# Row-sum and mean-square reciprocals: from VectorE's reciprocal to Exp of minus Ln on ScalarE

## The reference, cut to what matters

```python
def attn(x, gamma, w_qkv, w_out):          # layers 0 and 1
    ...
    qkv = jnp.einsum('bnc,fc->bnf', xn, w_qkv)
    ...
    sim = jnp.where(causal_mask, neg, jnp.einsum('bihd,bjhd->bhij', q, k))
    attn = jax.nn.softmax(sim, axis=-1)    # row sums: the first changed reciprocal
    out = jnp.einsum('bhij,bjhd->bihd', attn, v)
    return jnp.einsum('bnf,cf->bnc', out.reshape(b, n, 1024), w_out)

def L1_ffn(x, ...):                        # last stage, three blocks
    for blk in range(3):
        y = qlora_linear(h, ...)           # base + bias + LoRA
        mu = mean(y); var = mean((y - mu) ** 2)
        y = (y - mu) * rsqrt(var + 1e-5) * g + b   # the second changed one
        y = jax.nn.gelu(y, approximate=False)
        h = qlora_linear(y, ...) + h
    return h

x = x + layernorm(attn0(layernorm(x)))
x = x + layernorm(int8_matmul(layernorm(x)))
x = x + layernorm(attn1(layernorm(x)))
x = x + layernorm(L1_ffn(layernorm(x)))
```

## Time and profile before

| what | us |
|---|---|
| three runs | 4528.47, 4347.83, 4516.64 |
| median | 4516.64 |
| profiled execution, its own time | 4341.71 |
| its span on the slowest core (6) | 4340.2 |
| spans of the eight cores | 4296.7 to 4340.2 |
| attention of layer 0, phase B with its last out_groups | about 565 to 1590 |
| attention of layer 1, the same | about 2375 to 3376 |
| last stage | 3376 to 4340 |

### The profile page before, as it was taken

How to read it: one execution, slowest core, us unless ns; L and a number is a source line. 1 busy time by engine, 2 the same in 40 slices (tenths; PEclk the granted TensorE clock), 3 DMA queues, 4 the chain that set the end, 5 groups by cost and what they waited for, 6 DMA issues and landing times.

```text
span 4340.2 us, 45815 instructions; the slowest of 8 cores (4296.7 to 4340.2 us)
## 1 busy us (share of the span) xinstructions
PE 3411.5 (79%) x16411; PEld 1414.8 (33%) x16736; DVE 2637.4 (61%) x4777; ACT 2032.6 (47%) x2339; POOL 906.7 (21%) x868
## 2 busy tenths in 40 slices
PE   4888946787999945548998467899897379978997
PEld 1333322232333312223443123333332134433443
DVE  5666457666644458865555676655444466586457
ACT  1111113466777726662333135667784255436443
POOL 2222200000011003225565000000000123234333
PEclk8878767899999968778999689999998689989999
DMA  5111021113111044426566111111101500031004
GB/s 171 49 49 59 15 92 49 49 59 85 58 48 48 31 133 144 140 76 172 177 176 181 53 62 51 44 44 40 39 20 38 197 25 25 15 135 50 1 1 146
DMA packets 93476, 330.50 MB, mean 76 GB/s; under 512 B 12416, under 2 KB 16000, under 8 KB 88384
## 3 DMA queue, kind: packets, MB, share of 16 engines
q1 hardware_dynamic: 93248, 327.56, 22.9%
HBM read 228.94 MB, written 98.57 MB: 75 GB/s over the span
## 4 chain that ended last, share of the span: by engine, by line
PE 52%; DVE 35%; ACT 6%; DMA 3%; issue 3%; SPq 0%; POOL 0%; DVEq 0%; POOLq 0%; ACTq 0%; another core or an unknown queue 0%
PE pp L764 8%; PE pp L649 8%; PE pp L790 8%; DVE s_rcp L830 6%; PE pp L853 6%; PE pp L654 5%; PE pp L1316 4%; PE pp L807 3%; PE pp L1271 3%; ACT f_yg L1303 2%; PE pp L633 1%; DVE s_bst L859 1%; DVE s_y L860 1%; DVE s_x L866 1%; DVE f_r L1295 1%
## 5 line engine op out<-in xcount | busy, mean ns | idle before, releaser
L773 ACT ACTIVATE s_probs<-pp,s_negM 128x1024 bf16<-128x1024 f32 (+2 forms) x1152 | 1141.7, 1040 | 772.8 <-PE pp L764 765.2
L790 PE MATMUL pp<-s_probs,s_v 128*128 128x512 bf16 (+3 forms) x2271 | 667.5, 376 | 91.8 <-DVE s_feat L832 78.5
L764 PE MATMUL pp<-s_q,s_kT 128*128 128x512 bf16 (+3 forms) x2219 | 664.9, 380 | 31.2 <-DMA s_q<-qspill 17.0
L830 DVE RECIPROCAL s_rcp<-pp 128x512 f32<-128x512 f32 x128 | 429.7, 3357 | 126.3 <-PE pp L827 122.2
L780 POOL TENSOR_SCALAR_AFFINE_SELECT s_probs<-s_probs 128x256 bf16<-128x256 bf16 x256 | 107.9, 422 | 1682.8 <-ACT s_probs L773 1671.2
L853 PE MATMUL pp<-s_wq,s_feat 128*128 128x512 bf16 x1003 | 290.4, 439 | 153.2 <-DVE s_rcp L830 96.1
L1271 PE MATMUL pp<-f_h,f_w 128*128 128x512 bf16 x1501 | 364.3, 390 | 16.1 <-ACT f_h L1246 13.9
L807 PE MATMUL pp<-s_probs,ones 128*32 128x512 bf16 (+4 forms) x2302 | 247.1, 384 | 126.1 <-DVE s_lo L820 124.3
L790 PEld LDWEIGHTS pp<-s_probs,s_v 128*128 128x128 bf16 x2304 | 225.3, 101 | 355.9 <-DVE s_feat L832 91.6
L1281 POOL TENSOR_TENSOR f_sq<-f_yg 128x512 bf16<-128x512 bf16 x192 | 210.6, 1097 | 579.4 <-ACT f_yg L1276 573.3
L764 PEld LDWEIGHTS pp<-s_q,s_kT 128*128 128x128 bf16 x2304 | 195.7, 102 | 323.9 <-issue 128.3
(11 more groups left out here) (182 smaller groups left out, 5168.4 us busy)
## 6 DMA issues: line engine op xcount, KB each, us to landing
s_x<-x SPq DMA_DIRECT2D x64, 512.0 KB, 4.0
xbuf<-s_x SPq DMA_DIRECT2D x64, 512.0 KB, 2.6
s_fqi<-qwT SPq DMA_DIRECT2D x48, 512.0 KB, 5.1
s_fsc<-scT SPq DMA_DIRECT2D x48, 512.0 KB
qspill<-s_qst SPq DMA_DIRECT2D x16, 1024.0 KB, 7.1
s_q<-qspill SPq DMA_DIRECT2D x16, 1024.0 KB, 4.9
m_x<-xbuf SPq DMA_DIRECT2D x32, 512.0 KB, 5.0
xbuf<-m_x SPq DMA_DIRECT2D x32, 512.0 KB, 2.6
```

The costliest lines, as they stand in the source:

```text
L764: s_tok[i] = PE(lambda e, kc=kc, q0=q0, c0=c0, b=b, h=h, qt=qt: e.matmul(PS[b][:, c0:c0 + 512 - q0], S.kT[:, h, kc * 128:(kc + 1) * 128], ...
L773: tok = AC(lambda e, b=b, w=w, sl=sl, h=h, qt=qt: e.activation(S.probs[:, sl, 0:w], PS[b][:, 0:w], AF.Exp, bias=S.negM[:, h, qt:qt + 1], s ...
L790: tok = PE(lambda e, kc=kc, q0=q0, c0=c0, sl=sl, h=h, po=po, first=first, last=last: e.matmul(po[:, q0:512], S.v[:, kc, h * 128:(h + 1) * ...
L830: r = DV(lambda e: e.reciprocal(S.rcp[:, k, :], MISC), t)
```

## The change

The row sums' reciprocal leaves DVE: ACT takes Ln of MISC into `rcp`, then Exp with scale -1 in place. MISC is free after Ln. The multiply into `feat` waits for Exp. In the last stage Sqrt becomes Ln and the DVE reciprocal becomes ACT's Exp with scale -0.5; the multiplies wait for it. Both new instructions of the attention stand in ACT's queue between exp(i) and exp(i + 1) of the step in which `later` runs.

```diff
@@ -827,10 +827,10 @@
             t = PE(lambda e: e.matmul(MISC, w, lo, start=False, stop=True, skip_group_check=True),
                    inc=True)
             hl_free[k] = t
-            r = DV(lambda e: e.reciprocal(S.rcp[:, k, :], MISC), t)
-            st["misc"] = r
+            l = st["misc"] = AC(lambda e: e.activation(S.rcp[:, k, :], MISC, AF.Ln), t, po_free[k], A_mm)
+            r = AC(lambda e: e.activation(S.rcp[:, k, :], S.rcp[:, k, :], AF.Exp, scale=-1.0), l)
             f = DV(lambda e: e.tensor_mul(S.feat[:, qt % 2, h, :], PO[k], S.rcp[:, k, :]),
-                   av, feat_free[qt % 2])
+                   av, feat_free[qt % 2], r)
             po_free[k] = f
             st["feat", qt] = f
         return later
@@ -1291,15 +1291,15 @@
             for o in range(NF - 3, NF):
                 t = stat(o, sqt[o])
             S["st_free"] = a = AC(lambda e: e.activation(
-                rs, ST, AF.Sqrt, bias=M.epscol[:], scale=1.0 / D), t, S["r_free"][k], ("vc", p.vc))
-            DV(lambda e: e.reciprocal(rs, rs), a)
+                rs, ST, AF.Ln, bias=M.epscol[:], scale=1.0 / D), t, S["r_free"][k], ("vc", p.vc))
+            S["r_ok"] = AC(lambda e: e.activation(rs, rs, AF.Exp, scale=-0.5), a)
 
         def act(ocs):
             for oc in ocs:
                 n = S["nu"] % 2
                 S["nu"] += 1
                 d = DV(lambda e, oc=oc, n=n: e.tensor_mul(F.u[:, n, :], F.yg[yb][:, oc, :], rs),
-                       S["u_free"][n])
+                       S["u_free"][n], S["r_ok"])
```

## The result

The changed kernel is slower: the ratio to the kernel before is **1.0321, 95% interval 1.0287 to 1.0355**. The median of its four runs is 4484.83 us (4474.85 to 4870.61) against 4432.24 us for four runs of the kernel before; the two medians contain executions in which a die ran at a lower clock, which the ratio leaves out. The profiled execution took 4474.85 us (before: 4341.71), its slowest core is core 2 with a span of 4473.3 us.

The account below looks back on a forecast made before the run. PE was taken as the bound (TensorE busy 79%). Net idle of 67.0 us a layer x 1.38, 185 us for both, less 8 in the last stage: 4341.7 + 185 - 8 = 4519 us; own range 4460 to 4600, wider 4390 to 4720.

Parts of the forecast that it names:

- The mechanism: Attention: Ln waits for the MISC matmul, the next exponential stands behind the pair, and PE loses 2.65 us a head.
- The three output groups: Attention, steps 21, 33 and 407 of a layer: projection directly behind the pair waits for Ln only, 0.85 us each.
- What I credited as removed: Attention: PE waits tied to DVE's reciprocal that vanish, 76.0 us a layer together, 38.2 of them in tiles 2 to 7.
- Tile 0's seven heads: First query tile of each layer: a head's ring falls from 8.33 to 6.6 us, saving 12 us a layer.
- clock factor: Attention: each us of added PE idle costs 1.38 us through a lower granted clock; bounds 1.0 to 1.6.
- the end: End of each attention layer, where all wait for the last head: 3.36 becomes 1.26, saving 2.1 us.
- three such places: Start of the last stage: the reciprocal stands before statistics that PE's transposes need; 2.7 us each, -8 us.
- in steady state there is nothing to win: Last stage beyond its start: no PE wait ends with the reciprocal, so removing it gains nothing.
- Two tables: Attention: Ln and Exp need different tables, each pair swaps twice; +226 us, 4745 us in all; chance 0.12.
- The low part vanishes: Attention: waits for the sums' low part, 38.7 us a layer, go too; -107 us, 4412 us; chance 0.13.
- The lead survives: Attention: the pair costs PE nothing, only the 76.0 us a layer gain is seen; -218 us, 4124 us; chance 0.07.
- The break-even of 73 us a layer: Attention: 1.4 us a head, from (76.0 - 2.6) / 53; a pair holding PE for less makes the change a gain.

Follow-up runs that it names:

- e3: Kernel before plus two unused 512-column Copies on ScalarE where Ln and Exp would stand, both waiting for the second MISC matmul: ratio 1.0671.
- e4: Kernel before plus two unused 512-column Copies on ScalarE where Ln and Exp would stand, without waiting for the MISC matmul: ratio 1.0049.
- e5: Changed kernel with Ln, Exp and the multiply emitted one step later, at once if an output group comes first: ratio 0.9758.
- e6: Changed kernel with Ln, Exp and the multiply emitted two steps later in tiles 1 to 7, one in tile 0: ratio 0.9528, profiled 4107.9 us.
- e7: Kernel before with only the last stage changed, but Exp at scale +0.5 and DVE's reciprocal back in all 24 mean squares: ratio 1.0024, last stage 963.4 us.

## Why the prediction was right, and where it was not

**The mechanism.** Right, in place, size and count. The stall was put at 2.60 us by the clock of PE's issue, and it is 2.58. 53 heads a layer were to pay in full besides tile 0's seven; the trace of layer 0 has 60 such stalls at L764, each of 2.25 us or more. The three output groups that follow the pair directly wait for Ln alone, 0.75 us each (forecast 0.85). e3 makes the same stall with no Ln in it, e4 takes the wait out and the stall is gone, e5 and e6 shrink it by moving the pair.

**The sizes.** Ln 0.60 (597 ns), Exp 0.60 (629 ns). What I credited as removed has gone, down to L853's last 4.5 us. Tile 0's seven heads save 17 us, 5.9 us a head and not 6.6; with its clock factor the forecast had 12 x 1.38 = 16.6 for them. The granted clock there rose from 0.59 (590 to 650 us before) to 0.74 (585.3 to 620.5 after). By tiles, as medians over the eight cores, layers 0 and 1 against the forecast times 1.38: tile 0 -17 and -17 (-17), tile 1 -9 and -9 (-8), tiles 2 to 7 +116 and +126 (+120), the end -3 and -4 (-3).

In tiles 2 to 7 the product is right, but its two factors are not, and that is partly luck. On core 2 of layer 0 PE's idle time grew from 98 to 165 us, 67 us where the forecast had 87, because the view books 2.41 us of each stall as idle and 10 us of waits for POOL's mask went too (14.5 to 4.3 us on this core). Its busy time grew by 46 us for the same matmuls, 0.7 for each us of idle added, where the forecast took 0.38 from the average of the stretch before. The average after, 0.10 x 727 = 73 us on 165, is 0.44; what one more us of idle costs lies above either average. Some 8 of the 46 us are the stalls' own 0.17 us that the view counts as busy. In layer 1 POOL's mask held PE for only 0.8 us in tiles 2 to 7, before and after (core 2); in layer 0 it was 4 to 15 us before, by core. That may be why layer 0 lost less, 116 against 126; no run shows it apart. The range had a slip: 2.5 to 3.0 us a head and factors of 1.0 to 1.6 give 4452 to 4607, not 4460 to 4600.

**The last stage.** This is the term that was mis-sized: "three such places, 2.7 us each: -8 us", and "in steady state there is nothing to win". It gave -33 us. I looked for PE waits that end with the reciprocal, found none, and took the reciprocal to be free outside the start. But DVE hardly ever releases PE there in its own name: it releases ScalarE (`f_prep`, `f_yf`), which releases PE. Groups of PE and ScalarE in the last stage, core 2, kernel before:

```profile
L1345 PE MATMUL pp<-f_w,f_yg 128*128 128x512 bf16 x512 | 131.4, 403 | 14.6 <-ACT f_yf L1365 14.5
...
L1240 PE MATMUL pp<-ident_bf,f_prep 128*128 128x128 bf16 x256 | 25.6, 259 | 107.7 <-ACT f_prep L1231 88.9 <-ACT f_h L1246 18.9
...
L1365 ACT ACTIVATE f_yf<-pp,f_rr 128x512 f32<-128x512 f32 x64 | 46.3, 773 | 124.6 <-DVE f_rr L1362 124.6
L1231 ACT ACTIVATE f_prep<-f_xp,f_cf 128x1024 bf16<-128x1024 f32 x32 | 39.7, 1239 | 191.7 <-DVE f_cf L1229 191.7
```

and the changed kernel:

```profile
L1345 PE MATMUL pp<-f_w,f_yg 128*128 128x512 bf16 x512 | 129.8, 399 | 6.5 <-ACT f_yf L1365 6.5
...
L1240 PE MATMUL pp<-ident_bf,f_prep 128*128 128x128 bf16 x256 | 23.8, 248 | 93.8 <-ACT f_prep L1231 83.0 <-ACT f_h L1246 10.8
...
L1365 ACT ACTIVATE f_yf<-pp,f_rr 128x512 f32<-128x512 f32 x64 | 46.3, 773 | 114.2 <-DVE f_rr L1362 114.2
L1231 ACT ACTIVATE f_prep<-f_xp,f_cf 128x1024 bf16<-128x1024 f32 x32 | 39.6, 1239 | 168.8 <-DVE f_cf L1229 168.8
```

ScalarE's waits for DVE's row constants fall by 23 us (L1231) and 10 us (L1365). Behind them L1240's waits for f_prep and f_h fall by 14 us and L1345's for f_yf by 8. PE's busy time in the stage falls by 10 us with the same matmuls, at a granted clock of 0.93 for 0.92. e7 shows that these are DVE's: with its 3.35 us back, ScalarE's side unchanged, the stage is at 963 us. The condition I had set for being wrong here ("the last stage changed by more than 20 us") was met.

**The rivals.** Two tables: fallen, no load at the pair. The low part vanishes: fallen, L807 waits 130.8 us for it in both layers, 138.6 in e6. The lead survives: fallen for this kernel, but e6 is the kernel in which it nearly does, and it measures 0.953 where I had put that rival at 4124 us, 0.950. That the two are so close is luck: the attentions gave 170 us where the rival had 210, the last stage 34 where it had 8. The break-even of 73 us a layer fits too: e5, with a stall of 63 us a layer in place of 145, has attentions 70 us shorter than the kernel before, in sum.

**The sum.** 4341.7 + 185 - 8 = 4519 us was forecast; 1.0321 x 4341.7 = 4481, and the profiled execution took 4475. Of the difference of 38 to 44 us, 25 are the last stage's, 4 the attentions' (181 for 185), 5 lie in the stretches that the change doesn't touch, and the rest, some 10, is the difference between medians over cores, as in the table (together +143), and the slowest core (4474.85 - 4341.71 = +133).

## What to carry to other kernels

An instruction moved to an engine with idle time costs at most its length if it waits for nothing when it gets there; otherwise its wait holds up all that stands behind it. Ask who needs that: here 1.2 us of work cost 0.1 us a head without a wait and some 2.5 us with one, as the next instruction of PE needed the one behind it. If the work must move to an in-order engine that runs ahead, emit it later, behind what the bounding engine will need before the work's input is ready (here two steps), and flush it before a consumer that cannot wait. And for what an engine's work is worth, follow waits through the engine in the middle: who releases the one that releases PE.

## What the runs showed of the hardware

Exp and Ln ran from one loaded table: the Ln of the last stage's first mean square needed no load, as the attention had left a table with it behind (23 loads at L1293 for 24 before). Layer 0 ran all its work, Copy, Exp and Ln, on the load at L585, and layer 1 its exponentials and Ln on the one at L773. The Trainium skill ("ScalarE: Activation LUTs", Table sets: the hidden batching unit) says that one load serves Ln then Exp, and the trace agrees. Without a pointer operand an activation of 512 columns cost the same for the functions seen here: Ln from PSUM 597 ns, as Copy, Exp and Copy within SBUF 629. Ln with the pointer bias in the last stage took 687 ns, as Sqrt had the earlier trace rows. DVE's reciprocal of the same columns is 3357 ns, 5.6 times that.
